# An attention and expert kernel whose loops over batches and over expert tiles are written out as straight code

## The reference, cut to what matters

```python
# x: (16, 256, 128); 16 heads of 8; 8 experts, 128 -> 512 -> 128
h = layernorm(x)
Q, K, V = (einsum('bsd,hkd->bhsk', h, W) for W in (WQ, WK, WV))
scores = einsum('bhqd,bhkd->bhqk', Q, K) / sqrt(8)        # causal: -inf above the diagonal
y = einsum('bhsv,hdv->bsd', softmax(scores) @ V, WO)
x = x + layernorm(y)

t = layernorm(x).reshape(-1, 128)                          # 4096 tokens
aff = t @ centroids.T                                      # (4096, 8)
e = argmax(aff, axis=1); alpha = sigmoid(aff[e])           # one expert for each token
ye = t + relu(layernorm(t, ln_g[e], ln_b[e]) @ w1[e].T + b1[e]) @ w2[e].T + b2[e]
x = x + layernorm(alpha * ye + (1 - alpha) * t)
```

## Time and profile before

| what | value |
|---|---|
| median of 3 runs | 561.53 us |
| the 3 runs | 557.7, 561.53, 565.01 us |
| span of the profiled execution | 559.6 us |
| mean granted TensorE clock, share of full speed | 0.879 |
| DVE busy | 369.9 us (66%) |
| PE busy | 391.9 us (70%) |
| POOL busy | 250.3 us (45%) |
| DMA bytes moved | 39.96 MB |

### The profile page before, as it was taken

The page is one execution under the profiler, slowest core; times in us unless marked ns, Lnnn a source line. Parts: engine busy times, 40 slices in busy tenths (PEclk is TensorE's granted clock), DMA queues, the critical chain, the costliest instruction groups (busy, mean ns, idle before and its releaser), DMA issues.

```text
span 559.6 us, 13677 instructions
## 1 busy us (share of the span) xinstructions
PE 391.9 (70%) x3737; PEld 307.1 (55%) x3738; DVE 369.9 (66%) x1422; ACT 251.1 (45%) x548; POOL 250.3 (45%) x349
## 2 busy tenths in 40 slices
PE   3287769679679797797796796874196768776630
PEld 2155547557457576575575574653185557665530
DVE  7568558578586586687786775876465666666650
ACT  2125445446445454454554553641074555554520
POOL 5612444343445544535545444565214444444453
PEclk9999789899798798898998887995589997899985
DMA  6635454254252352342451442121321111111100
GB/s 181 119 50 86 110 95 83 74 96 73 38 97 61 59 86 72 54 86 62 67 86 50 74 82 69 57 101 39 126 68 56 59 50 56 46 56 53 57 18 5
DMA packets 33398, 39.96 MB, mean 71 GB/s; under 512 B 7561, under 2 KB 27149, under 8 KB 31808
## 3 DMA queue, kind: packets, MB, share of 16 engines
q1 hardware_dynamic: 28400, 32.02, 28.4%
q0 software_dynamic: 2832, 6.53, 3.4%
q10 hardware_dynamic: 2112, 0.80, 0.8%
HBM read 25.18 MB, written 14.61 MB: 71 GB/s over the span
## 4 chain that ended last, share of the span: by engine, by line
PE 35%; DMA 24%; POOL 13%; issue 11%; DVE 9%; ACT 2%; DVEq 1%; POOLq 1%; ACTq 1%; SPq 1%
DMA shift_rows<-nmT 17%; POOL out_x L521 7%; PE ST L819 5%; PE O L840 4%; DMA aug<-shift_rows 4%; POOL rsz L529 4%; PE S L806 3%; PE M L852 3%; PE S L799 2%; PE S L796 2%; PE M L867 2%; PE ST L828 2%; PE O L844 2%; PE S L801 2%; DMA aug<-qk_parts 2%
## 5 line engine op out<-in xcount | busy, mean ns | idle before, releaser
L1060 DVE TENSOR_REDUCE nmf<-S 128x2 f32<-128x512 f32 (+1 forms) x192 | 130.8, 683 | 91.6 <-PE S L799 58.0
L592 ACT ACTIVATE p<-ST 128x1024 f32<-128x1024 f32 x64 | 65.7, 1027 | 58.3 <-PE ST L819 57.6
L819 PE MATMUL ST<-aug 128*128 128x256 bf16 x256 | 43.6, 299 | 57.5 <-DMA aug<-shift_rows 57.5
L429 POOL TENSOR_SCALAR_AFFINE_SELECT p<-p 128x512 f32<-128x512 f32 x64 | 41.0, 640 | 91.5 <-ACT p L592 91.3
L521 POOL DMA_INDIRECT out_x<-vaug,ids x39 | 40.3, 1034 | 72.8 <-DVE vez L1403 68.8
L819 PEld LDWEIGHTS ST<-aug 128*128 128x128 bf16 x256 | 24.4, 104 | 63.3 <-issue 35.4
L806 PE MATMUL S<-aug 126*128 126x128 bf16 x512 | 53.9, 231 | 0.0
L433 POOL TENSOR_SCALAR_AFFINE_SELECT p<-p 128x512 f32<-128x512 f32 x64 | 41.6, 649 | 19.9 <-ACT p L596 17.1
L990 PE MATMUL O<-w_tab,vaug 128*128 x312 | 45.6, 292 | 0.8 <-ACT vaug L729 0.8
L806 PEld LDWEIGHTS S<-aug 126*128 126x128 bf16 x512 | 43.2, 105 | 4.4
L840 PE MATMUL O<-p,vaug 128*32 128x256 f32 x512 | 44.1, 414 | 0.9 <-POOL p L429 0.9
(11 more groups left out here) (149 smaller groups left out, 950.8 us busy)
## 6 DMA issues: line engine op xcount, KB each, us to landing
qk_parts<-qkp SPq DMA_DIRECT2D x16, 384.0 KB, 2.8
aug<-qk_parts SPq DMA_DIRECT2D x32, 192.0 KB
x_all<-xs_rows SPq DMA_DIRECT2D x39, 131.0 KB, 2.1
aug<-qk_parts SPq DMA_DIRECT2D x32, 128.0 KB
aug<-qk_parts SPq DMA_DIRECT2D x32, 64.0 KB
w_tab<-in_w1t SPq DMA_DIRECT2D x8, 256.0 KB, 2.6
w_tab<-in_w2t SPq DMA_DIRECT2D x8, 256.0 KB, 3.1
out_x<-vaug,ids POOLq DMA_INDIRECT x39, 2.3
```

Of the source, the lines that this page charges most:

```text
L429: g.affine_select(out=v, in_=v, compare_op=ALU.is_ge, fill=0.0, base=0, pattern=[[0, 4], [1, P]], channel_multiplier=-1).then_inc(s["sel0" ...
L592: a.activation(p0[:, gr % 2], ST0[:, :, :], ACT.Exp, scale=SCALE).then_inc(s["exp0"], 1)
L819: last = mm(ST0[:, j], kaug[:, p, h, 0:P], qaug[:, p, h], start=True, stop=True)
L1060: v.tensor_reduce(dst, S[:, n % 2].rearrange("p (j n) -> p j n", j=k), op=ALU.max, axis=AX_X, negate=True).then_inc(s["red"], 1)
```

## The change

Both loops go, and SP's loop over tiles too: every step is written out, on every engine, with numbers for indices and for the values to wait for. `wait_fixed` goes with them, and with it the additional wait for `consts`; each place waits with `wait_ge` for a constant. `kept` has the plain step number as its key, and `add_bias` takes the register from it without a case for a missing entry. What is computed, the order of the steps, the buffers and the DMAs stay.

```diff
@@ class Nth
-        return a * self.k + b if self.trip is None else self.trip * (self.unroll * a) + (a * self.k + b)
+        return a * self.k + b
@@ iterations
-            first = UB + 1
-            trips = (B - 3 - first) // UB
-            for i in range(first):
+            for i in range(B + 4):
                 step(Nth(i))
-            with eng.Fori(0, trips) as trip:
-                for k in range(UB):
-                    step(Nth(first + k, trip, UB))
-            for i in range(first + trips * UB, B + 4):
-                step(Nth(i))
@@ tiles
-            first = 5
-            trips = (ST - 3 - first) // UT
-            for k in range(-3, first):
+            for k in range(-3, ST + 3):
                 step(Nth(k))
-            with eng.Fori(0, trips) as trip:
-                for k in range(UT):
-                    step(Nth(first + k, trip, UT))
-            for k in range(first + trips * UT, ST + 3):
-                step(Nth(k))
@@ parts_out (and likewise in 22 other places)
-                wait_fixed(sp, s["parts_d"], b.times(1, 1))
+                sp.wait_ge(s["parts_d"], b.times(1, 1))
                 if b.follows(RING):
-                    wait_fixed(sp, aug_in[p], b.turns(RING, 96))
+                    sp.wait_ge(aug_in[p], b.turns(RING, 96))
@@ SP's rows_in
-            for t in range(UT):
-                rows_in(Nth(t))
-            trips = ST // UT - 1
-            with sp.Fori(0, trips) as trip:
-                for k in range(UT):
-                    rows_in(Nth(UT + k, trip, UT))
-            for t in range(UT * (trips + 1), ST):
+            for t in range(ST):
                 rows_in(Nth(t))
@@ weights, add_bias, tile_step on DVE
-                e = kept[id(t.trip), t.k]
+                e = kept[t.k]
...
-                e = kept.pop((id(t.trip), t.k), None)
-                if e is None:
-                    e = expert(dve, t)
+                e = kept.pop(t.k)
...
-                    kept[id(n.trip), n.k] = expert(dve, n)
+                    kept[n.k] = expert(dve, n)
```

More of the change, by code:

```diff
@@ L274, in tile @@
             n = t.plus(stage)
-            return n if t.trip is not None or 0 <= n.k < ST else None
+            return n if 0 <= n.k < ST else None
         def expert(eng, t):
@@ L312, in parts_in @@
                 p = b.slot(RING)
-                wait_fixed(sp, qk_w[p], b.turns(RING, 16, 16))
+                sp.wait_ge(qk_w[p], b.turns(RING, 16, 16))
                 if b.follows(RING):
-                    wait_fixed(sp, s["st1_r"], b.times(NG, -NG * (RING - 1)))
+                    sp.wait_ge(s["st1_r"], b.times(NG, -NG * (RING - 1)))
                 row = 0
@@ L327, in shift @@
                 p = b.slot(RING)
-                wait_fixed(sp, sh_w[half], b.times(16, 16))
+                sp.wait_ge(sh_w[half], b.times(16, 16))
                 if b.follows(RING):
-                    wait_fixed(sp, s["st1_r"], b.times(NG, -NG * (RING - 1)))
+                    sp.wait_ge(s["st1_r"], b.times(NG, -NG * (RING - 1)))
                 sp.dma_start(qaug[SHIFT:P, p, 8 * half:8 * half + 8],
@@ L352, in step @@
                     shift(b, 0)
-                if i.trip is None and i.k <= B:
+                if i.k <= UB or B + 1 - E + UB < i.k <= B:
                     e = i.k if i.k <= UB else i.k - (B + 1 - E)
@@ L442, in number @@
             def number(b):
-                wait_fixed(pool, s["x2_d"], b.times(1, 1))
+                pool.wait_ge(s["x2_d"], b.times(1, 1))
                 g.tensor_copy(pay[:, b.slot(RING), :, TOK].bitcast(I32), b.pick(tokid, 2, 2)).then_inc(s["id_in"], 1)
@@ L450, in scatter @@
                 if t == 0:
[L451 to L454, removed]
+                    pool.wait_ge(s["ln_sh"], b.times(1, 1))
+                    pool.wait_ge(s["id_in"], b.times(1, 1))
+                    pool.wait_ge(s["al_d"], b.times(1, 1))
+                    pool.wait_ge(s["pos_d"], b.times(1, 1))
                 g.indirect_dma_start(out=xs_dram, out_offset=bass.IndirectOffsetOnAxis(ap=pos[:, p, t:t + 1].bitcast(U32), axis=0),
@@ L519, in leave @@
                 p = t.slot(2)
-                wait_fixed(pool, s["zo_d"], t.times(1, 1))
+                pool.wait_ge(s["zo_d"], t.times(1, 1))
                 g.indirect_dma_start(out=out.rearrange("b t d -> (b t) d"),
@@ L527, in power_z @@
                 p = t.slot(2)
-                wait_fixed(pool, s["ve_z"], t.times(1, 1))
+                pool.wait_ge(s["ve_z"], t.times(1, 1))
                 g.tensor_tensor(rsz[:, p:p + 1], vez[:, p:p + 1], mhalf[:, 0:1], op=ALU.pow).then_inc(s["rs_z"], 1)
@@ L569, in shift_out @@
                 a.activation(nmT[:, p, half], M[:, 0:P // 2].bitcast(BF16)[0:32, 0:P], ACT.Copy).then_inc(s["sh_d"], 1)
-                wait_fixed(act, s["sh_d"], b.times(2, half + 1))
+                act.wait_ge(s["sh_d"], b.times(2, half + 1))
                 if b.follows(RING):
-                    wait_fixed(act, sh_in[half], b.times(16, -16 * (RING - 1)))
+                    act.wait_ge(sh_in[half], b.times(16, -16 * (RING - 1)))
                 act.dma_start(sh_dram[p, half].rearrange("c (r t) -> (c r) t", t=P), nmT[:, p, half])\
@@ L1098, in ln_stats @@
             def ln_stats(b, n):
-                wait_fixed(dve, s[("y_d", "x2_d", "f_d")[n]], b.times(1, 1))
+                dve.wait_ge(s[("y_d", "x2_d", "f_d")[n]], b.times(1, 1))
                 for t in (0, 1):
@@ L1104, in ln_aggregate @@
             def ln_aggregate(b, n):
-                wait_fixed(dve, s["ln_st"], b.times(3, n + 1))
+                dve.wait_ge(s["ln_st"], b.times(3, n + 1))
                 for t in (0, 1):
@@ L1166, in alphas @@
                 else:
-                    wait_fixed(dve, s["al_p"], b.times(1, 1))
+                    dve.wait_ge(s["al_p"], b.times(1, 1))
                     v.reciprocal(pay[:, b.slot(RING), :, ALPHA], b.pick(eneg, 2, 2)).then_inc(s["al_d"], 1)
@@ L1186, in place @@
                 if n == 2:
-                    wait_fixed(dve, s["pf_d"], b.times(1, 1))
+                    dve.wait_ge(s["pf_d"], b.times(1, 1))
                     v.tensor_copy(pos[:, b.slot(RING)], b.pick(posf, 2, 2)).then_inc(s["pos_d"], 1)
```

31 lines of the change are left out of this document (10 added, 21 removed).

## The result

| | before | changed |
|---|---|---|
| median of 4 runs, us | 562.02 (557.7 to 565.01) | 536.33 (533.51 to 540.64) |
| span of the profiled execution, us | 559.6 | 534.6 |
| mean granted TensorE clock | 0.879 | 0.904 |
| first to last output scatter, us | 419.7 to 552.4 | 406.6 to 527.4 |
| loads of the expert on DVE | 51 | 39 |

The ratio in paired rounds is 0.9655 [0.9588, 0.9722]; the medians of the table give 0.954. The forecast was 14.0 us, 547.5 us, with a range of 540 to 555 us; the ratio times the 561.5 us of before is 542 us.

The account below looks back on a forecast made before the run. Bounds: a ring through SP and small DMAs in the attention stage, a POOL and DVE ring in the expert stage. 9.3 + 0.5 + 2.2 + 3.5 - 1.5 = 14.0 us gained, giving 547.5 us, range 540 to 555.

Parts of the forecast that it names:

- (d): SP in the attention stage: shorter delays at its reads, `parts_out` and `parts_in` save 3.5 us, bounds 0 and 3.5.
- (e): Straight code must be read: some 10 more 16 KB transfers in batches 7 to 12 lose 1.5 us, bounds 0 to 5.1.
- (a): Expert stage, DVE: `add_bias` no longer loads the expert a second time in 12 tiles; saves 9.3 us, bounds 5.9 and 9.3.
- (c): Expert stage, POOL: the `consts` wait ahead of the scatter goes, 0.06 us a tile; saves 2.2 us, bounds 0 and 2.2.
- (b): Turns of the loops: those over tiles save 0.5 us together; nothing counted for those over batches.
- the ring: Attention stage: first scores, shift, SP's reads, `parts_out`, `parts_in` and small DMA set each step's period, 21.7 us.
- Code comes late: Rival: PE and ACT stop in batches 7 to 12 for code queued behind `qk_parts`, up to 6 us each; 576 us, 3%.
- Only the tiles gain: Rival: DMA traffic sets the attention stage or code reading eats its gain; 10 us remain, 551.5 us, chance 23%.
- The second load isn't the cause: Rival: a slow phase of PE at each trip's start makes the long tiles; 4.7 us go, 556.8 us, chance 7%.
- The turns cost more: Rival: two turns over batches each hold a ring engine 1.5 us; attention stage gives 3 us more, 544.5 us, 4%.

Follow-up runs that it names:

- e1: Changed kernel with the second load of the expert put back in add_bias in 12 steps; 550.89 us, ratio 0.9733 to the kernel before.
- e2: Changed kernel, all loops written out, but wait_fixed kept with its wait for `consts`; 552.14 us, ratio 0.9774 to the kernel before.
- e4: Kernel before with only the batches written out; loop over tiles, second loads and `consts` waits kept; 559.5 us, ratio 0.9916 to the kernel before.
- e11: e2 plus 12 matmuls with overwritten result where PE waits for half 0; 543.63 us, ratio 0.9619 to the kernel before.
- e12: Changed kernel plus 12 matmuls with overwritten result where PE waits for half 0; 534.89 us, ratio 0.9505 to the kernel before.
- e7: Kernel before, loops and `consts` waits kept, plus 12 matmuls with overwritten result where PE waits for half 0; 548.07 us, ratio 0.9799 to the kernel before.
- e8: The changed kernel itself, timed again with no further edit; 540.36 us, ratio 0.962 to the kernel before.
- e10: Changed kernel with the loop over batches put back on PE alone, no added matmuls; 537.55 us, ratio 0.9599 to the kernel before.
- e9: e10 plus 12 matmuls with overwritten result where PE waits for half 0; 529.69 us, ratio 0.9424 to the kernel before.
- e3: Changed kernel with `consts` waits and the loop over batches kept on all engines, only the tiles written out; 556.19 us, ratio 0.9859 to the kernel before.

## Why the prediction was right, and where it fell short

The direction was right, and so were the two main mechanisms, the second load and the shorter handovers. The paired ratio puts the time at 542 us, inside the range of 540 to 555; the median of the runs, 536.3 us, is 3.7 us under its low end. The gain was 19 to 21 us for a forecast of 14.0. The tiles gave what was forecast, and the excess is in the attention stage: (d) and (e) were both sized too low and nearly cancel, which is luck, and the clock of PE, which has no term in the sum, gave 6.0 us in the two profiles.

- **(a) second load, 9.3 us: right.** The four long stretches fell from 48.65 to 38.84 us, 9.8 with some 0.7 of `consts` in it, so 9.1. There are 39 loads, and no group of three takes over 10 us. e1 shows the cause.
- **(c) `consts` on POOL, 2.2 us: right.** e2 puts it at 1.8.
- **(b) turns, 0.5 us: wrong.** The stage lost 11.9 us where (a) to (c) say 12.0, but not at the turns. The 0.33 us that the first stretch of five tiles has over 16.40 is one tile of 3.61 us, the fourth of the five, and the changed kernel has 3.59 at the same place with no loop. Its three stretches of five take 16.46, 16.22 and 16.10 us: 0.27, 0.26 and 0.38 less, of which `consts` is 0.30 each. e4 keeps the loop and has 3.28 for every one of these tiles. So a turn costs nothing that shows, and the sum of the stage agrees because the tail gave what (b) was to give (one of the last tiles went from 3.34 to 2.92). In the changed kernel's tile of 3.59 us DVE stood 0.33 us between `z_bias` and `add_bias` with no wait; what held it was not looked into.
- **(d) SP in the attention stage, 3.5 us with a bound of 3.5: too small.** The handovers lost 6.4 us in steps 4 to 12 and about 0.2 a step in the straight ones. Three things made it small. I measured steps in the loop against straight steps of the same kernel, which had waits for `consts` as well, and gave one such wait a step to SP where the ring has several (landing to read is now 0.02 us, not the 0.05 of a straight step before). I took SP alone, while ACT's issue (0.07 a step) and PE's first scores (0.12) are in the same ring. And I put the bound at the value itself, so nothing above it was in the range. e11 against e12 puts `consts` alone at some 4 us here, 2.8 of them in the handovers. And "every delay on SP in this ring is paid in full" holds for the handover itself, but with the matmuls in both kernels (e7 and e12) the steps as a whole came out no shorter.
- **Not foreseen: the clock of PE.** I read it in the tiles, to exclude it, and not in the attention stage, where the earlier trace rows have 0.89, 0.88 and 0.91. In steps 4 to 12 the stretch behind the wait ran at 0.76 in place of 0.57, 6.0 us in these two profiles (e8, the same kernel, has 0.66, and 3.1 us). That such a change of clock makes such a change of time is shown by e7. That the shorter wait (3.16 against 3.74 us) is what raised it is not shown, and e10 speaks against the wait's length alone: its wait is shorter still, 2.75 us, and its clock there is 0.69. What raised the clock stays open.
- **(e) more code, 1.5 us lost: right in kind.** 11 more q8 transfers came, at the places named. The mechanism is not an engine that waits for code but a small DMA that lands later beside a transfer. e9 and e10 put 2 to 5 us on reading PE's code. So 1.5 was low, and inside its bound of 5.1. Of the 5.0 us by which two landings grew in the table of the ring, `parts_out` has 1.7, in steps with a q8 transfer beside it; the 3.2 of half 0 can't be put down to code, since e3 and e7, whose PE loops, have 8.52 and 8.34 us there, like the changed kernel's 8.35, though e10 has 8.00. What made it grow stays open.
- **Steps 0 to 3**, straight in both kernels, became 3.5 us shorter (84.8 to 81.3 us), and what lies ahead of them 0.8. Handovers explain about 0.8 of it. The rest is no steady gain: e8 and e1, with the same code there, take 84.1 and 84.6 us.

The rivals. *Code comes late*: no stop of PE or ACT for code was seen, and the longest delay of a small DMA was 2.2 us. *Only the tiles gain*: refuted for the change as it stands, 19 to 21 us by the ratios against 11.9 in the tiles, and e4 is faster than before with the tiles' loop kept. With the 12 matmuls in both kernels it is not refuted: 16 us by the runs, uncertain by 6, and nothing outside the tiles in the traces. *The second load isn't the cause*: refuted by e1. *The turns cost more*: its 544.5 us is near the ratio's 542, but not for its reason. e3 keeps these turns and is 4.8 us over e2, which also holds all the register work of the loop; the earlier trace rows have 0.21 us for a turn, and e4's tiles show nothing at theirs. The Trainium skill (Runtime: NRT & Kernel Launch, section Instruction fetch mechanics) says that a taken branch whose target lies outside the engine's window of code makes it fetch before it can go on; nothing here shows a fetch at the turns.

## What to carry to other kernels

Follow a ring through every engine that hands work on, and count on each of them the satisfied waits and the registers computed behind a wait: 0.04 to 0.2 us each made some 7 us in the attention stage here. Take the baseline for such a term from an ideal handover (landing to read 0.02 us), not from another step of the same kernel, and leave room above the value. And before a gain is put down to the edit, bring the clock of PE to the same level in both kernels and read it: a few matmuls in its wait nearly did that here (1.00 and 0.98), and were worth 2.0% by themselves in the kernel before. Take more than one profile of the same kernel before a few us of one are explained; here three of the same code lay 5 us apart.

## What the runs showed of the hardware

- PE's granted clock behind a wait of PE was 0.50 in some steps and 1.00 in others, and 22 matmuls then took 3.84 us or 2.04. The length of the wait alone didn't decide: in steps 4 to 12 of the changed kernel it was 0.50 behind 4.20 and 3.25 us and 1.00 behind 2.02, 2.59, 2.74 and 3.36 us. Six matmuls in the wait did as well as twelve (0.9493, 0.9523).
- One code transfer of 16 KB beside an 8 KB DMA made it land 1.2 to 2.2 us later (2.49 to 3.51 us against 1.34), with little other traffic on the 16 engines, where it began before the last packets of that DMA. Where it began behind them it cost nothing (1.34 us in e10).
- A satisfied wait cost 0.04 to 0.07 us at a place of the ring. Loading a register from a table took 0.30 us and the register operation behind it 0.19, and with the gaps around them they put 0.64 us between two dependent steps of DVE (e1).
